# A spike-train feed-forward on one NeuronCore: 96 instead of 128 places for general tokens, and a second layer in which w2 stands still

## The chip, the core and the metric

The kernel runs on one core of a Trainium2 chip (trn2). The metric is device time in microseconds (us); a smaller number is better. Engines are named as the profile names them: PE is the matrix engine (TensorE), PEld its weight loads, DVE is VectorE, ACT is ScalarE, POOL is GpSimd, SP is SyncE, which here issues the plain transfers.

## The reference

The input x has 2 sequences of 2048 tokens and 512 channels. Each channel keeps a running sum; a spike of height 1000 stands where the sum passes a whole number. The spikes go through a two-layer network, and the result is added to x:

```
rates = relu(x) * 0.001
c     = cond[:, None, :] + cumsum(rates, axis=1)
spikes = (floor(c) - floor(previous c)) / 0.001
h     = relu(spikes @ w1 + b1)        # 512 -> 2048
out   = x + h @ w2 + b2               # 2048 -> 512
```

All data are float32. The sums here rise by less than two, so nearly all tokens have no spike at all, some have one, and few have several.

## The kernel before, in words

The kernel does not run the network over all 4096 tokens. It sorts tokens into three kinds.

**Idle tokens** have no spike. Their network output is one and the same row, `idle_row`; it is added to x in place by DVE and POOL (`add_idle`), and SP stores the result (`store_idle`).

**Single tokens** have one spike, in one channel. PE builds a table with the output row of every channel (`table_chunk`, 16 chunks of w1 and w2, a sum of 64 matmuls of 512 columns); POOL adds the rows onto the stored output with eight scattered accumulating transfers (`add_row`).

**General tokens** have spikes in several channels. DVE gives each of them a place, 1 to 128, in `hot` and `slot` (`find_slots`, `first_spikes`, `second_spikes`); PE then has the spikes of all places as `spk_t`, with 4 pieces of 128 channels on the partitions and the 128 places as columns. These places go through the network as one tile:

- `first_layer` on PE: for each of 16 pieces of 128 hidden units (`m`), 4 matmuls, w1 as the standing operand (128 by 128), the spikes as the moving one (128 columns). The results alternate between two PSUM tiles, `ps_turn` and `ps_small`; ACT turns each into `hidden[m]` (`relu_hidden`).
- `sum_checks` on PE, one small matmul with 2 moving columns: it counts the general tokens and odd cases for `judge` on DVE. If there were more general tokens than places, a slow loop over all tokens would follow (`redo`); it does not run on this input.
- `second_layer` on PE: 16 matmuls, `hidden[m]` as the standing operand and 512 columns of w2 as the moving one, summed in `ps_out`. The places stand on the partitions of the result, so that it can be used row by row.
- DVE adds x and b2 of those tokens (gathered by POOL into `general_x`) in one operation on `ps_out`, and POOL scatters the rows into the output.

The order on each engine is that of the code; there is no scheduler. Semaphores connect the engines: `spk_ready` (DVE to PE), `hidden_summed` and `hidden_ready` (PE to ACT and back), `out_summed` (PE to DVE), `row_ready` (DVE to POOL). SP ends the program when all stores and scatters have landed. The scatter names a row far outside the output for each empty place, and such rows are not written (`bounds_check`).

The last steps stand in the code like this:

```
            dve.wait_ge(out_summed, 1)
            dve.tensor_tensor(new_row, ps_out[:, :], general_x[:, :], ALU.add).then_inc(row_ready, 1)
...
            pool.wait_ge(row_ready, 1)
            pool.indirect_dma_start(out=out_rows, out_offset=bass.IndirectOffsetOnAxis(ap=to_general[:, :], axis=0),
```

The functions that the change touches, and what calls them:

Of the kernel before, what the change touches and what calls it, by code (L numbers as in the profile page):

```python
# [6 lines left out]
ALU = mybir.AluOpType  # L7
# [11 lines left out]
def spike_ffn(nc, x, x_turned, cond, cond_cols, w1, w_pairs, b1_cols, b2, out):  # L19
# [23 lines left out]
    NOT_FIRST = 1024.0  # L43
    assert BLK == 16 and D == 512 and B == 2 and F == 2048
# [10 lines left out]
    with ExitStack() as ctx:  # L55
# [22 lines left out]
        hot = sb("hot", [P, NE, P])  # L78
# [65 lines left out]
        new_row = w_sb[:, 8, 0, :]  # L144

# [27 lines left out]
        ps_checks = ps_table[DC - 1]  # L173

# [52 lines left out]
        hidden_ready = sem("hidden_ready")  # L227
        out_summed = sem("out_summed")
# [82 lines left out]
        def _(pool):  # L311
# [55 lines left out]
            for b in range(B):  # L367
                if b == 1:
                    pool.wait_ge(general_listed, 1)
                    pool.indirect_dma_start(out=general_x[:, :], out_offset=None, in_=x_rows,  # L370
                                            in_offset=bass.IndirectOffsetOnAxis(ap=from_general[:, :], axis=0)
                                            ).then_inc(general_got, 16)
# [8 lines left out]
            pool.indirect_dma_start(out=out_rows, out_offset=bass.IndirectOffsetOnAxis(ap=to_general[:, :], axis=0),  # L381
                                    in_=new_row, in_offset=None, bounds_check=last_row, oob_is_err=False
# [26 lines left out]
        def _(act):  # L409
# [40 lines left out]
            def relu_hidden(m, summed, count, ready):  # L450
                act.wait_ge(summed, count)
                act.activation(hidden[m], ps_hidden[m % 2][:, 0:P], ACT.Relu,  # L452
                               bias=b1_col[:, m:m + 1], scale=PER_DT).then_inc(ready, 1)

            for m in range(FC):
                relu_hidden(m, hidden_summed, m + 1, hidden_ready)
                if 1 <= m <= DC:
                    act.activation(table_row[m - 1], ps_table[m - 1][:, :], ACT.Copy).then_inc(table_rows_ready, 1)

            act.wait_ge(redo_ready, 1)  # L460
            redo = redo_count(act)
            with act.If(redo > 1):
                for b in range(B):
                    with act.Fori(1, redo) as tile:
# [3 lines left out]
                        for m in range(FC):  # L468
                            relu_hidden(m, again_hidden_summed, tile * FC + (b * BLK * FC - FC + m + 1),
                                        again_hidden_ready)  # L470
# [5 lines left out]
        def _(dve):  # L476
# [137 lines left out]
            def find_slots(b):  # L614
# [4 lines left out]
                chain(dve.tensor_tensor(hot[:, mine, :], over(slot[:, mine], P), along(slot_name[:, :], DC), ALU.is_equal))  # L619
# [7 lines left out]
            def first_spikes():  # L627
                dve.wait_ge(slots_found, 1)
                chain(dve.tensor_tensor(spk_t[:, :, :], over(token[:, own(0)], P), along(ps_slots[:, 0:P], DC), ALU.is_equal))  # L629

            def second_spikes():
                dve.wait_ge(slots_found, 2)
                for c in range(DC):
                    last = dve.scalar_tensor_tensor(out=spk_t[:, c, :], in0=ps_slots[:, P:2 * P],  # L634
                                                    scalar=token[:, DC + c:DC + c + 1], in1=spk_t[:, c, :],
# [17 lines left out]
            def list_general():  # L653
                for b in range(B):
                    chain(dve.scalar_tensor_tensor(out=diagonal[:, :], in0=ps_slots[:, b * P:(b + 1) * P], scalar=1.0,
                                                   in1=ident[:, :], op0=ALU.mult, op1=ALU.mult, accum_out=slot_rows[:, b:b + 1]))
                chain(dve.tensor_tensor(slot_row[:, :], slot_rows[:, 0:1], slot_rows[:, 1:2], ALU.add))
                chain(dve.tensor_scalar(none_far[:, :], slot_row[:, :], 0.5, FAR, ALU.is_lt, ALU.mult))
                dve.tensor_scalar(from_general[:, :], slot_row[:, :], -1.0, 0.0, ALU.add, ALU.max)
                dve.scalar_tensor_tensor(out=to_general[:, :], in0=slot_row[:, :], scalar=-1.0, in1=none_far[:, :],  # L660
                                         op0=ALU.add, op1=ALU.add).then_inc(general_listed, 1)

            def judge():
                dve.wait_ge(checks_summed, 1)
                chain(dve.tensor_scalar(crowd[:, :], ps_checks[:, 0:1], P + 0.5, None, ALU.is_gt))  # L665
# [61 lines left out]
            chain(dve.tensor_tensor(general_x[:, :], general_x[:, :], b2_row[:, :], ALU.add))  # L727
            dve.wait_ge(out_summed, 1)
            dve.tensor_tensor(new_row, ps_out[:, :], general_x[:, :], ALU.add).then_inc(row_ready, 1)  # L729
# [62 lines left out]
        def _(pe):  # L792
# [80 lines left out]
            def find_slots(b):  # L873
# [3 lines left out]
                for c in range(DC):  # L877
                    col = b * DC + c
                    last = pe.matmul(ps_slots[:, b * P:(b + 1) * P], token[:, col:col + 1].to_broadcast([P, P]),
# [3 lines left out]
            def first_layer(ready, base):  # L883
# [59 lines left out]
            with pe.If(redo > 1):  # L943
                pe.wait_ge(row_ready, 1)
                for b in range(B):
# [5 lines left out]
                    with pe.Fori(1, redo) as tile:  # L951
# [6 lines left out]
                        for last in first_layer(again_hidden_ready, base):  # L958
# [34 lines left out]
```

## Time and profile before

| | |
|---|---|
| time, three runs | 103.97, 103.45, 103.96 us; median 103.96 us |
| span of the profiled execution | 102.1 us; the timed runs are 1.3 to 1.9 us longer than this span |
| PE busy | 95.4 us (93% of the span), 370 records |
| PEld busy | 54.0 us (53%) |
| DVE busy | 65.9 us (64%) |
| ACT busy | 35.5 us (35%) |
| POOL busy | 43.2 us (42%) |
| mean granted TensorE clock | 0.991 |

The span runs from the first to the last instruction of the profiled execution; no separate device time is listed for that execution, so its span stands beside the runs. Each float32 matmul of the program leaves two records in the trace, each with a weight load of its own; a transpose leaves one. The end of a matmul record is modelled, so the distance from one start to the next says more of PE's pace than the length of a record.

### The profile page before, as it was taken

How to read it: one execution, taken by the hardware profiler on the slowest of the kernel's cores; microseconds unless marked ns; L12 is line 12 of the kernel's file. 1: busy time of each engine (PE TensorE's matmuls, PEld its weight loads, DVE VectorE, ACT ScalarE, POOL GpSimd, SP SyncE). 2: the span in 40 equal slices, each digit the busy share in tenths (PEclk: the TensorE clock that was granted, in tenths of full speed). 3: DMA queues.
4: the chain of work that ended last, by engine and by line, in shares of the span. 5: the costliest groups of instructions: out<-in, count | busy, mean ns of one | idle time of the engine just before them, and what ended most of it. 6: DMA issues, size and time to landing. Idle time of an engine off the chain costs nothing.

```text
span 102.1 us, 1157 instructions
## 1 busy us (share of the span) xinstructions
PE 95.4 (93%) x370; PEld 54.0 (53%) x370; DVE 65.9 (64%) x142; ACT 35.5 (35%) x64; POOL 43.2 (42%) x44
## 2 busy tenths in 40 slices
PE   5999999999999999999969999999999999999910
PEld 5944444444644444644234564649999984444300
DVE  2448999888699999488958888899993020020020
ACT  2796515315372540569740000003953330000000
POOL 6350000000078700017508181499937883688040
PEclk9999999999999999999999999999999999999996
DMA  1999999999999999999999725427999999998701
GB/s 58 286 387 414 417 420 411 411 407 409 409 409 409 396 393 401 409 394 387 379 373 352 324 116 218 193 125 292 395 430 436 407 336 195 218 115 106 92 8 62
DMA packets 10028, 31.66 MB, mean 310 GB/s; under 512 B 1671, under 2 KB 1799, under 8 KB 8994
## 3 DMA queue, kind: packets, MB, share of 16 engines
q1 hardware_dynamic: 8304, 29.63, 74.7%
q0 software_dynamic: 1568, 1.90, 11.4%
q8 instruction: 5, 0.08, 0.3%
q14 instruction: 5, 0.04, 0.1%
q10 hardware_dynamic: 146, 0.01, 0.1%
HBM read 21.58 MB, written 10.75 MB: 316 GB/s over the span
## 4 chain that ended last, share of the span: by engine, by line
PE 50%; DVE 20%; POOL 13%; issue 11%; ACT 1%; POOLq 1%; DVEq 0%
PE ps_table L807 40%; DVE x_sb L673 11%; POOL out L347 11%; PE ps_small L900 4%; DVE same L600 3%; PE ps_idle L823 2%; PE ps_turn L844 2%; DVE hot L619 1%; PE ps_idle L827 1%; PE ps_idle L833 1%; DVE spk_t L634 1%; POOL out L381 1%; POOL general_x L370 1%; POOLq L258 1%; DVE spk_t L629 1%
## 5 line engine op out<-in xcount | busy, mean ns | idle before, releaser
L807 PE MATMUL ps_table<-w_sb 128*128 128x512 f32 x128 | 56.9, 595 | 0.0
L807 PEld LDWEIGHTS ps_table<-w_sb 128*128 128x128 f32 x128 | 23.6, 190 | 27.1 <-issue 26.4
L342 POOL DMA_INDIRECT rates<-in_x_turned,sixteen_at x8 | 9.9, 1236 | 33.9 <-DVE sixteen_at L563 32.1
L354 POOL TENSOR_TENSOR x_sb<-x_sb,idle_row 128x512 f32<-128x512 f32 x12 | 14.9, 1277 | 9.9 <-DVEq L706 3.7
L422 ACT ACTIVATE w_sb<-w_sb,b_col 128x512 f32<-128x512 f32 (+2 forms) x19 | 12.2, 643 | 16.5 <-DMA w_sb<-in_w_pairs 16.3
L549 DVE SCALAR_TENSOR_TENSOR total_two<-x_sb,total_two 128x1024 f32<-128x1024 f32 x14 | 17.1, 1225 | 1.2 <-DMA x_sb<-in_x 0.8
L347 POOL DMA_INDIRECT out<-w_sb,to_single x8 | 12.5, 1558 | 5.8 <-issue 3.7
L895 PE MATMUL ps_table<-w_sb 128*128 128x512 f32 x32 | 14.0, 595 | 0.0
L423 ACT ACTIVATE w_sb<-w_sb,minus_relu_b 128x512 f32<-128x512 f32 (+2 forms) x19 | 12.3, 649 | 0.6
L673 DVE TENSOR_TENSOR x_sb<-x_sb,ps_idle 128x2048 f32<-128x2048 f32 x5 | 11.2, 2283 | 1.5 <-ACT idle_row L448 1.3
L895 PEld LDWEIGHTS ps_table<-w_sb 128*128 128x128 f32 x32 | 6.0, 190 | 7.2 <-issue 6.9
L452 ACT ACTIVATE w_sb<-ps_turn,b_col 128x128 f32<-128x128 f32 x8 | 2.9, 367 | 19.0 <-PE ps_turn L888 18.4
L888 PE MATMUL ps_small<-spk_t,w_sb 128*128 128x128 f32 x64 | 8.5, 275 | 0.0
L888 PE MATMUL ps_turn<-spk_t,w_sb 128*128 128x128 f32 x64 | 8.5, 275 | 0.0
L888 PEld LDWEIGHTS ps_turn<-spk_t,w_sb 128*128 128x128 f32 x64 | 7.9, 192 | 0.5 <-DVE spk_t L634 0.3
L888 PEld LDWEIGHTS ps_small<-spk_t,w_sb 128*128 128x128 f32 x64 | 7.8, 192 | 0.0
L509 DVE SCALAR_TENSOR_TENSOR idle_part<-w_sb,relu_b,idle_part 128x512 f32<-128x512 f32 x9 | 6.7, 750 | 1.5 <-DMA w_sb<-in_w_pairs 1.4
L729 DVE TENSOR_TENSOR w_sb<-ps_table,general_x 128x512 f32<-128x512 f32 x1 | 0.7, 692 | 6.3 <-PE ps_table L895 6.3
L900 PE MATMUL ps_small<-ones 128*128 128x128 f32 x16 | 3.7, 427 | 1.1 <-POOLq L320 1.1
L727 DVE TENSOR_TENSOR general_x<-general_x,b_row 128x512 f32<-128x512 f32 x1 | 0.7, 691 | 6.2 <-DMA general_x<-in_x,from_general 6.2
L900 PEld LDWEIGHTS ps_small<-ones 128*128 128x128 f32 x16 | 3.5, 330 | 1.1 <-POOLq L320 1.1
L665 DVE TENSOR_SCALAR crowd<-ps_table 128x1 f32<-128x1 f32 x1 | 0.2, 159 | 6.1 <-PE ps_table L871 6.1
(113 smaller groups left out, 65.5 us busy)
## 6 DMA issues: line engine op xcount, KB each, us to landing
x_sb<-in_x SPq DMA_DIRECT2D x16, 512.0 KB, 14.3
out<-x_sb SPq DMA_DIRECT2D x8, 1024.0 KB, 4.1
w_sb<-in_w_pairs SPq DMA_DIRECT2D x15, 512.0 KB, 15.7
w_sb<-in_w SPq DMA_DIRECT2D x4, 1024.0 KB, 15.3
w_sb<-in_w_pairs SPq DMA_DIRECT2D x2, 256.0 KB, 2.9
b_row<-in_b SPq DMA_DIRECT2D x1, 256.0 KB, 15.3
rates<-in_x_turned,sixteen_at POOLq DMA_INDIRECT x8, 6.5
out<-w_sb,to_single POOLq DMA_INDIRECT x8
```

What stands on the lines that cost most here:

```text
L342: pool.indirect_dma_start(out=rates[:, col, :], out_offset=None, in_=x_sixteen, in_offset=bass.IndirectOffsetOnAxis(ap=sixteen_at[:, col:c ...
L347: pool.indirect_dma_start(out=out_rows, out_offset=bass.IndirectOffsetOnAxis(ap=to, axis=0), in_=row, in_offset=None, bounds_check=last_ro ...
L354: last = pool.tensor_tensor(x_sb[b][:, t, :], x_sb[b][:, t, :], idle_row[:, :], ALU.add)
L422: chain(act.activation(weights, weights, ACT.Relu, bias=b1_col[:, m:m + 1], scale=PER_DT))
L423: act.activation(weights, weights, ACT.Identity, bias=minus_relu_b1[:, m:m + 1]).then_inc(table_hidden_ready, 1)
L509: step = dve.scalar_tensor_tensor(out=idle_part[:, :], in0=w2_sb[:, m, :], scalar=relu_b1[:, m:m + 1], in1=idle_part[:, :], op0=ALU.mult, ...
L549: chain(dve.scalar_tensor_tensor(out=total_two[b][:, :, :], in0=tokens, scalar=0.0, in1=total_two[b][:, :, :], op0=ALU.max, op1=ALU.add))
L673: last = dve.tensor_tensor(tokens, tokens, along(ps_idle[:, :], end - begin), ALU.add)
L807: last = pe.matmul(ps_table[c][:, :], table_hidden[:, m, c * P:(c + 1) * P], w2_sb[:, m, :], start=(m == 0), stop=(m == FC - 1))
L888: last = pe.matmul(ps_hidden[m % 2][:, 0:P], w1_sb[:, c, m * P:(m + 1) * P], spk_t[:, c, :], start=(c == 0), stop=(c == DC - 1))
L895: last = pe.matmul(ps_out[:, :], hidden[m], w2_sb[:, m, :], start=(m == 0), stop=(m == FC - 1))
L900: pe.matmul(ps_small[:, 0:P], ones[:, :], ones[:, :], start=True, stop=True)
```

## The change

General tokens get 96 places (`SLOTS`) instead of 128. Every operation on places has 96 columns or 96 partitions: `hot`, `spk_t`, the moving columns of `find_slots` and `first_layer`, `relu_hidden`, the gather into `general_x`, the list of rows, and the scatter. `judge` sends more than 96 general tokens into the slow loop.

The second layer is turned round. In `general_layer` a piece of w2 (128 hidden units by 128 output channels) stands still and `hidden[m]` moves with 96 columns: four sums of 16 matmuls, one for each 128 output channels, in four PSUM tiles. The results have the channels on the partitions. ACT copies each to `out_turned[c]`, and PE turns it back with a transpose (`turn_out`), three of them into `ps_out` and the last into another tile, `ps_out_last`. DVE adds x and b2 in two pieces of 384 and 128 channels.

```diff
+    SLOTS = 96
...
+        out_turned = [w_sb[:, 9, 0, c * SLOTS:(c + 1) * SLOTS] for c in range(DC)]
...
+        ps_out_turned = [ps_table[1], ps_table[2], ps_turn, ps_small]
+        ps_out_last = ps_table[1]
...
             for m in range(FC):
-                relu_hidden(m, hidden_summed, m + 1, hidden_ready)
+                relu_hidden(m, hidden_summed, m + 1, hidden_ready, SLOTS)
...
+            for c in range(DC):
+                act.wait_ge(out_turned_summed, c + 1)
+                act.activation(out_turned[c], ps_out_turned[c][:, 0:SLOTS], ACT.Copy).then_inc(out_turned_ready, 1)
...
-                chain(dve.tensor_tensor(hot[:, mine, :], over(slot[:, mine], P), along(slot_name[:, :], DC), ALU.is_equal))
+                chain(dve.tensor_tensor(hot[:, mine, :], over(slot[:, mine], SLOTS), along(slot_name[:, 0:SLOTS], DC), ALU.is_equal))
...
-            dve.wait_ge(out_summed, 1)
-            dve.tensor_tensor(new_row, ps_out[:, :], general_x[:, :], ALU.add).then_inc(row_ready, 1)
+            dve.wait_ge(out_summed, DC - 1)
+            most = slice(0, (DC - 1) * P)
+            chain(dve.tensor_tensor(new_row[0:SLOTS, most], ps_out[0:SLOTS, most], general_x[0:SLOTS, most], ALU.add))
+            dve.wait_ge(out_summed, DC)
+            rest = slice((DC - 1) * P, D)
+            dve.tensor_tensor(new_row[0:SLOTS, rest], ps_out_last[0:SLOTS, 0:P], general_x[0:SLOTS, rest], ALU.add).then_inc(
+                row_ready, 1)
...
-                        last = pe.matmul(ps_hidden[m % 2][:, 0:P], w1_sb[:, c, m * P:(m + 1) * P],
-                                         spk_t[:, c, :], start=(c == 0), stop=(c == DC - 1))
+                        last = pe.matmul(ps_hidden[m % 2][:, 0:n], w1_sb[:, c, m * P:(m + 1) * P],
+                                         spk_t[:, c, 0:n], start=(c == 0), stop=(c == DC - 1))
...
+            def turn_out(c):
+
+                pe.wait_ge(out_turned_ready, c + 1)
+                to = ps_out_last[0:SLOTS, 0:P] if c == DC - 1 else ps_out[0:SLOTS, c * P:(c + 1) * P]
+                pe.transpose(to, out_turned[c], ident[:, :]).then_inc(out_summed, 1)
+
+            def general_layer():
+
+                for c in range(DC):
+                    for m in range(FC):
+                        if c == 0:
+                            pe.wait_ge(hidden_ready, m + 1)
+                        last = pe.matmul(ps_out_turned[c][:, 0:SLOTS], w2_sb[:, m, c * P:(c + 1) * P], hidden[m][:, 0:SLOTS],
+                                         start=(m == 0), stop=(m == FC - 1))
+                    last.then_inc(out_turned_summed, 1)
+                    if c > 0:
+                        turn_out(c - 1)
+                turn_out(DC - 1)
...
-            for last in first_layer(hidden_ready, 0):
+            for last in first_layer(hidden_ready, 0, SLOTS):
                 last.then_inc(hidden_summed, 1)
             sum_checks()
-            second_layer(hidden_ready, 0).then_inc(out_summed, 1)
+            general_layer()
```

On PE, from the end of the first layer to the end of the second, the kernel before issues these rows (line, operation, the tile written and those read, partitions by columns, the semaphores waited for, how many in a row):

```order
L888 MATMUL ps_turn<-spk_t,w_sb 128x128 [waits hidden_ready]
L888 MATMUL ps_turn<-spk_t,w_sb 128x128 x3
L888 MATMUL ps_small<-spk_t,w_sb 128x128 [waits hidden_ready]
L888 MATMUL ps_small<-spk_t,w_sb 128x128 x3
L871 MATMUL ps_table<-checks,ones 128x2 [waits table_rows_ready,odd_ready]
L895 MATMUL ps_table<-w_sb 128x512 [waits hidden_ready] x16
```

The changed kernel issues these at the same place; the line numbers are its own, and `w_sb` holds w2, `hidden` and `out_turned`.

```order
L903 MATMUL ps_turn<-spk_t,w_sb 128x96 [waits hidden_ready]
L903 MATMUL ps_turn<-spk_t,w_sb 128x96 x3
L903 MATMUL ps_small<-spk_t,w_sb 128x96 [waits hidden_ready]
L903 MATMUL ps_small<-spk_t,w_sb 128x96 x3
L886 MATMUL ps_table<-checks,ones 128x2 [waits table_rows_ready,odd_ready]
L919 MATMUL ps_table<-w_sb 128x96 [waits hidden_ready] x16
L919 MATMUL ps_table<-w_sb 128x96 x16
L911 MATMUL ps_table<-ident,w_sb 96x128 [waits out_turned_ready]
L919 MATMUL ps_turn<-w_sb 128x96 x16
L911 MATMUL ps_table<-ident,w_sb 96x128 [waits out_turned_ready]
L919 MATMUL ps_small<-w_sb 128x96 x16
L911 MATMUL ps_table<-ident,w_sb 96x128 [waits out_turned_ready] x2
```

Sixteen matmuls with 512 columns became 64 with 96 columns and four transposes; two of the transposes stand between the sums, two behind the last.

On DVE, at the end of the program, the kernel before has these rows, from `judge` to the last addition:

```order
L666 TENSOR_TENSOR redo_f<-ps_table,crowd 128x1 [waits dve_step]
L667 TENSOR_SCALAR redo_f<-redo_f 128x1 [waits dve_step]
L668 TENSOR_SCALAR redo_i<-redo_f 128x1 [waits dve_step]
L727 TENSOR_TENSOR general_x<-general_x,b_row 128x512 [waits b2_in,general_got]
L729 TENSOR_TENSOR w_sb<-ps_table,general_x 128x512 [waits out_summed,dve_step]
```

The changed kernel has these there:

```order
L676 TENSOR_TENSOR redo_f<-ps_table,crowd 128x1 [waits dve_step]
L677 TENSOR_SCALAR redo_f<-redo_f 128x1 [waits dve_step]
L678 TENSOR_SCALAR redo_i<-redo_f 128x1 [waits dve_step]
L737 TENSOR_TENSOR general_x<-general_x,b_row 96x512 [waits b2_in,general_got]
L740 TENSOR_TENSOR w_sb<-ps_table,general_x 96x384 [waits out_summed,dve_step]
L743 TENSOR_TENSOR w_sb<-ps_table,general_x 96x128 [waits out_summed,dve_step]
```

The last addition is split in two, and only the second piece waits for the last transpose.

## Rows read from the trace of the kernel before

**Rows 1.** Busy time of each engine in three stretches, granted clock, DMA share.

```profile
core 0: us, PE busy (x) PEld busy (x) DVE busy (x) ACT busy (x) POOL busy (x), PEclk, DMA share, GB/s
...
68.50:83.20 14.70, 14.70 (x130) 14.46 (x129) 8.67 (x19) 7.47 (x19) 11.87 (x10) 1.00 0.97 391
83.20:97.40 14.20, 14.14 (x36) 6.14 (x34) 1.31 (x5) 0.37 (x1) 8.16 (x6) 1.00 0.89 153
97.40:102.10 4.70, 0.00 (x0) 0.00 (x0) 0.69 (x1) 0.00 (x0) 1.03 (x1) 0.80 0.10 37
```

**Rows 2.** Timeline of the last 5 us: start, length, engine, line, [idle before, releaser].

```profile
96.75 0.59 PE L895 MATMUL ps_table<-w_sb 128*128 128x512 f32 x1
97.45 0.69 DVE L729 TENSOR_TENSOR w_sb<-ps_table,general_x 128x512 f32<-128x512 f32 x1 [6.32 <-PE ps_table L895]
98.42 1.03 POOL L381 DMA_INDIRECT out<-w_sb,to_general  x1 [3.79 <-DVE w_sb L729]
```

**Rows 3.** Timeline of both layers on PE, PEld and POOL, merged runs of records.

```profile
68.52 0.19 PEld L888 LDWEIGHTS ps_turn<-spk_t,w_sb 128*128 128x128 f32 x1 [0.26 <-DVE spk_t L634]
68.93 1.05 PE L888 MATMUL ps_turn<-spk_t,w_sb 128*128 128x128 f32 x8
...
83.11 0.30 PEld L871 LDWEIGHTS ps_table<-checks,ones 128*128 128x128 f32 x2
83.22 0.28 PE L871 MATMUL ps_table<-checks,ones 128*128 128x2 f32 x2
83.33 0.30 PEld L895 LDWEIGHTS ps_table<-w_sb 128*128 128x128 f32 x2
83.36 13.98 PE L895 MATMUL ps_table<-w_sb 128*128 128x512 f32 x32
...
93.09 1.55 POOL L347 DMA_INDIRECT out<-w_sb,to_single  x1 [0.30 <-issue]
```

**Rows 4.** Timeline at `count_leads(1)`, where matmuls have one moving column.

```profile
62.23 1.02 PE L807 MATMUL ps_table<-w_sb 128*128 128x512 f32 x2
...
62.91 0.17 DVE L611 TENSOR_TENSOR_SCAN leads_run<-ones,leads 128x4 f32<-128x4 f32 x1
63.19 0.30 PEld L862 LDWEIGHTS ps_small<-leads_run,upper 128*128 128x128 f32 x2 [0.77 <-DVEq L612]
...
63.41 0.30 PEld L865 LDWEIGHTS ps_small<-leads_run,ones 128*128 128x128 f32 x2
63.63 0.30 PEld L807 LDWEIGHTS ps_table<-w_sb 128*128 128x128 f32 x2
```

**Rows 5.** The transposes of L856: duration ns min/median/max, first and last start.

```profile
L856 PEld LDWEIGHTS ps_met<-ident,token x4: 137/137/137, 47.2 to 47.9; 128*128 128x128 f32 x4
L856 PE MATMUL ps_met<-ident,token x4: 272/272/273, 47.7 to 48.0; 128*128 128x128 f32 x4
```

**Rows 6.** ACT by line and shape: busy us, mean ns of one.

```profile
L452 ACT ACTIVATE w_sb<-ps_small,b_col 128x128 f32<-128x128 f32 x8 | 2.9, 368 | 3.2 <-PE ps_small L888 2.6 <-issue 0.5
...
L458 ACT ACTIVATE w_sb<-ps_table 128x512 f32<-128x512 f32 x4 | 2.4, 590 | 0.0
...
L433 ACT ACTIVATE relu_b<-b_col 128x16 f32<-128x16 f32 x1 | 0.2, 216 | 0.4 <-DMA b_col<-in_b_cols 0.4
```

**Rows 7.** Timeline where PE waits for a copy of ACT.

```profile
51.34 0.60 ACT L446 ACTIVATE idle_base<-ps_idle 128x512 f32<-128x512 f32 x1 [0.91 <-PE ps_idle L827]
...
51.99 0.30 PEld L833 LDWEIGHTS ps_idle<-idle_base,strip_first 128*128 128x128 f32 x2 [1.63 <-ACT idle_base L446]
```

**Rows 8.** DVE by line and shape.

```profile
L619 DVE TENSOR_TENSOR hot<-slot,slot_name 128x512 f32<-128x512 f32 x2 | 1.4, 691 | 0.1
...
L665 DVE TENSOR_SCALAR crowd<-ps_table 128x1 f32<-128x1 f32 x1 | 0.2, 159 | 6.1 <-PE ps_table L871 6.1
```

**Rows 9.** DMA queue of POOL from 98.5 us to the end: packets, MB.

```profile
q0 software_dynamic: 80, 0.15, 10.8%
```

**Rows 10.** From the page's costliest groups, the first matmuls of the program.

```profile
L900 PE MATMUL ps_small<-ones 128*128 128x128 f32 x16 | 3.7, 427 | 1.1 <-POOLq L320 1.1
```

More of the change, by code:

```diff
@@ L77, in spike_ffn @@
         same = sb("same", [P, D], BF16)
-        hot = sb("hot", [P, NE, P])
+        hot = sb("hot", [P, NE, SLOTS])
         spk_t = sb("spk_t", [P, DC, P])
@@ L448, in _, with relu_hidden @@
             act.activation(idle_row[:, :], ps_idle[:, :], ACT.Copy).then_inc(idle_copied, 1)
[L450 removed]
+            def relu_hidden(m, summed, count, ready, n):
                 act.wait_ge(summed, count)
[L452 removed]
+                act.activation(hidden[m][:, 0:n], ps_hidden[m % 2][:, 0:n], ACT.Relu,
                                bias=b1_col[:, m:m + 1], scale=PER_DT).then_inc(ready, 1)
             for m in range(FC):
[L456 removed]
+                relu_hidden(m, hidden_summed, m + 1, hidden_ready, SLOTS)
                 if 1 <= m <= DC:
                     act.activation(table_row[m - 1], ps_table[m - 1][:, :], ACT.Copy).then_inc(table_rows_ready, 1)
+            for c in range(DC):
+                act.wait_ge(out_turned_summed, c + 1)
+                act.activation(out_turned[c], ps_out_turned[c][:, 0:SLOTS], ACT.Copy).then_inc(out_turned_ready, 1)
             act.wait_ge(redo_ready, 1)
@@ L628, in first_spikes @@
                 dve.wait_ge(slots_found, 1)
-                chain(dve.tensor_tensor(spk_t[:, :, :], over(token[:, own(0)], P), along(ps_slots[:, 0:P], DC), ALU.is_equal))
+                chain(dve.tensor_tensor(spk_t[:, :, 0:SLOTS], over(token[:, own(0)], SLOTS), along(ps_slots[:, 0:SLOTS], DC), ALU.is_equal))
             def second_spikes():
@@ L633, in second_spikes @@
                 for c in range(DC):
-                    last = dve.scalar_tensor_tensor(out=spk_t[:, c, :], in0=ps_slots[:, P:2 * P],
-                                                    scalar=token[:, DC + c:DC + c + 1], in1=spk_t[:, c, :],
+                    last = dve.scalar_tensor_tensor(out=spk_t[:, c, 0:SLOTS], in0=ps_slots[:, P:P + SLOTS],
+                                                    scalar=token[:, DC + c:DC + c + 1], in1=spk_t[:, c, 0:SLOTS],
                                                     op0=ALU.is_equal, op1=ALU.add)
@@ L878, in find_slots, with first_layer @@
                     col = b * DC + c
-                    last = pe.matmul(ps_slots[:, b * P:(b + 1) * P], token[:, col:col + 1].to_broadcast([P, P]),
+                    last = pe.matmul(ps_slots[:, b * P:b * P + SLOTS], token[:, col:col + 1].to_broadcast([P, P]),
                                      hot[:, col, :], start=(c == 0), stop=(c == DC - 1))
                 last.then_inc(slots_found, 1)
-            def first_layer(ready, base):
+            def first_layer(ready, base, n):
                 for m in range(FC):
@@ L957, in _ @@
                         base = tile * FC + (b * BLK * FC - FC)
-                        for last in first_layer(again_hidden_ready, base):
+                        for last in first_layer(again_hidden_ready, base, P):
                             last.then_inc(again_hidden_summed, 1)
```

29 lines of the change are left out of this document (16 added, 13 removed).

## The prediction

> **What bounds the kernel now.** I read the busy times by stretch first. From 68.5 to 97.4 us PE is busy in 28.84 of 28.9 us at a granted clock of 1.00, its full level; then it is silent, and DVE and POOL have one instruction each [rows 1]. The page's chain of work leads through POOL's single scatters instead; the timeline of the end corrects it. The last of these is issued at 93.09 and over at 94.64 [rows 3], but POOL's next scatter comes at 98.42 with an idle time put down to DVE's L729, which waited 6.32 us for PE's L895 [rows 2]. So the end is set by PE's two layers, then DVE's addition (97.45 to 98.14), then the last scatter. POOL has 94.64 to 98.14, 3.5 us, in hand.
>
> PE's first layer is not held up by what goes before on DVE: its first weight load, released by `spk_t`, starts at 68.52, and its first matmul at 68.93 [rows 3], a distance of 0.41 us, which is the length of the 512-column matmul still in the array (32 of them take 13.98 us to the end of the last [rows 3]; less 0.25 us of pipeline tail that is 0.43 each).
>
> **The price of a matmul with 96 columns** decides all. The rows give two candidates. By moving columns: a 512-column record takes 0.429 us, and a 128-column one (83.22 - 68.93) / 128 = 0.1116 us [rows 3]; the line through both gives 0.085 us at 96. By weight load: where the moving operand has one column (L862, L865), pairs of loads start at 63.19, 63.41 and 63.63, thus 0.11 us each [rows 4], and the two loads of L871 and those behind them, round matmuls of two columns, start 0.11 apart as well (83.11, 83.33) [rows 3]. Almost nothing moves there, and the pace is that of 128 columns. So a float32 load of 128 by 128 takes 0.111 us, one load runs beside one matmul, and 128 columns are just where both are equal. The change keeps every load at 128 by 128 and gives up only moving columns. I take 0.1115 us a record, with 0.109 as the low end (63.19 to 63.63 over four, read to 0.01 us, is 0.11).
>
> The Trainium skill (TensorE: Matmul & The Clock Gate, section Back-to-back issue gap) gives a rule for an isolated matmul in which the distance at full clock follows the moving columns with a small constant; by it one would go by the first candidate, and the sum below would be about 6 us lower on PE. The rows with one and two columns disagree with that here, since there is a weight load for every record; the page itself says that in a stream with loads both count.
>
> **First layer.** Same 128 records, same loads: 14.29 us before and after, gain 0. ACT's `relu_hidden` gets a little shorter (0.368 us at 128 columns [rows 6]) and is hidden, since a piece on PE lasts 8 x 0.1116 = 0.89 us. `find_slots` on PE also keeps its loads: 0.
>
> **Second layer.** Before: the stream takes 31 x 0.429 + 0.59 (the last record to its end) = 13.89 us from the first effective start at 97.34 - 13.89 = 83.45. (97.34 is 96.75 + 0.59 [rows 2]; the record itself starts at 83.36, ahead of its second load.) After: 64 matmuls, 128 records, 127 x 0.1115 = 14.16 us to the last start; two transposes stand among them, one record of 0.11 us each (four start between 47.7 and 48.0 [rows 5]), 0.22; and the last record to its end, 0.25 us (272 ns at 128 columns [rows 5], 32 fewer). Sum 14.63. **+0.74 us**; with 0.109 a record +0.42. The copies of the first three sums by ACT and their transposes lie under the next sum (16 x 2 x 0.1115 = 3.6 us): 0. All 16 `hidden` but the last are long ready.
>
> **Turning back, after the last sum ends.** Before: end of L895 at 97.34, DVE starts 0.11 later and takes 0.69: 0.80 us [rows 2]. After, two paths join. The last sum goes to ACT (0.04 us for the semaphore, my estimate, from the 0.05 between ACT's end at 51.94 and PE's load at 51.99 [rows 7]); a copy of 96 columns, which is between 216 ns (16 columns) and 368 ns (128 columns with a bias), by the line from 16 to 512 columns 0.28 us [rows 6]; 0.05 to PE [rows 7]; the transpose, 0.27 from matmul start to end plus about 0.06 of its load ahead (137 ns of record, half of it overlapping [rows 5]) = 0.33. Together 0.70. Meanwhile `turn_out(2)` comes 0.13 after the last sum; 0.11 later DVE starts on 384 columns, by the line from 159 ns for 1 to 691 for 512 columns [rows 8] 0.56 us, so it ends at 0.80. The last piece starts at about 0.81 by either path and takes 0.29 (128 columns on the same line): 1.10. **+0.30 us**; ends: copy 0.22 and all waits at their shortest +0.15; copy 0.37, and the chain's wait and the semaphores twice as long +0.65.
>
> **Start of the layers.** At 63.19 PE waits for DVE's `leads_ready`: its matmul L807 of 62.23 had streamed by 62.23 + 2 x 0.43 = 63.09, and the load of L862 starts 0.10 later and is not hidden [rows 4]. On DVE ahead of it stands `hot` for the first sequence, 4 x 128 columns in 691 ns [rows 8]; with 4 x 96 it is 128 x 1.04 = 0.13 us shorter. PE has about 0.10 of waiting and 0.11 of unhidden load to give back there. I take **-0.13 us**, from -0.20 to 0. The other shorter operations of DVE (`hot` for the second sequence, `spk_t`) finish `spk_t` some 0.4 us earlier, ahead of a PE that is the bound: 0.
>
> **The scatter.** It names 96 rows instead of 128, 1.03 us on POOL [rows 2]. No row shows one with fewer. If all of it goes by rows it is -0.26; if none, 0. **-0.10**, since the instruction has some fixed part. The transfer gains nothing: it moved 0.15 MB [rows 9], which is about 73 rows of 2 KB, so empty places are left out already, and it will be the same 73 rows. That number is also under 96, so the slow loop stays out. The gather for 96 rows ends long before it is needed: 0. Stores and single scatters have the 3.5 us in hand.
>
> **Sum.** +0.74 + 0.30 - 0.13 - 0.10 = +0.81 us. The profiled span of 102.1 becomes 102.9; the median of the runs, 103.96, lies 1.9 above the span, and I carry that over: **104.8 us**. With all terms at their ends the likeliest case goes from 103.96 + 0.42 + 0.15 - 0.20 - 0.26 = 104.1 to 103.96 + 0.74 + 0.65 = 105.4. What a measurement of this kernel can tell from no change is about 0.5%, 0.52 us, so "the same" is 103.4 to 104.5.
>
> **Rivals.**
> - *Moving columns set the pace.* Place: both layers. The first layer loses 128 x 0.0265 = 3.4 us; the second is 127 x 0.085 + 0.22 + 0.25 = 11.27 against 13.89, -2.6. The row would be ready about 5.8 us earlier, at 92.3; then POOL's last single scatter, over at 94.64, comes in between, and the gain ends at about 3.4 us: 100.5 us. It decides for faster as soon as a record falls below about 0.108 us in both layers. For it speaks that 0.1116 fits 128 columns as well; against it, all rows with one or two columns. 6 in 100.
> - *The clock falls.* PE then streams 96 columns in a record of 0.1115 us where it streamed 128, and no row shows what the clock does in such a stretch; it could be granted at its lower level, 1.2 GHz, in both layers. Against it: in this trace it fell only in the stretch in which PE is silent (0.80 on average [rows 1]), and the loads go on without a gap. The first matmuls of the program, of the same shape, took 3.7 us for 16 [rows 10], 0.23 each; at that price 256 records take 59 instead of 28.5 us: some 130 us. 2 in 100.
> - *The turned layer costs no more than it gives.* The same mechanism as the forecast, but the small gains are at their far ends (a scatter priced by rows, -0.26, PE's bubble fully gone, -0.20, a copy of 0.22 us): 104.1 to 104.5. 17 in 100.
>
> The forecast, load-bound with a sum over 0.52 us, keeps 75. Of the rivals the first is faster, the third the same, the second slower: faster 0.07 (with a little for an unseen gain), same 0.17, slower 0.76. The range of 104.0 to 105.5 is the likeliest case's own with its ends and 0.1 at either side, as the runs shown lie 0.5 us apart; it takes in the third rival. What is outside is the first two and terms that I have missed, together under 2 in 10.
>
> **What would show it.** In the changed profile the matmuls of the first layer should start 0.111 to 0.112 us apart, 8 in 0.89 us, as before; those of the second likewise, 16 matmuls in 3.57 us; PE's start of the first layer at about 68.8; the end of the last sum at about 97.95; ACT's copies of 0.25 to 0.37 us; the last transpose some 0.7 us behind the last sum; DVE's last piece at an end of about 99.05; the scatter 0.9 to 1.03 us. The prediction is wrong if a load with 96 moving columns behind it goes faster than one with 1 or 128, if the clock row shows less than 1.00 between 68 and 98 us, or if transposes among the matmuls hold up the stream by more than their 0.11 us.

## The result and the profile after

The changed kernel took 105.58 us (median; 105.17 to 105.86), beside 103.97 us for the kernel before: ratio 1.0171, interval 1.0111 to 1.0232. Three later comparisons of the same two kernels gave 1.0126 (1.0070 to 1.0182), 1.0108 (1.0070 to 1.0147) and 1.0111 (1.0049 to 1.0173). Ratios leave out slow executions (here one of the kernel before, of 207.75 us), which the medians, here and below, take in. The change makes the kernel 1.1 to 1.7% slower; 0.8 us, 0.8%, was forecast, with a range that ended at 105.5 us. The profiled execution has its own time here, 105.17 us, with a span of 103.4 us.

The stretches of the changed kernel that answer to [rows 1], cut where its own layers begin and end (busy us and number of records of each engine, granted clock, DMA share, GB/s):

```profile
68.50:82.80 14.30, 14.30 (x130) 14.30 (x129) 7.94 (x19) 7.07 (x19) 12.08 (x9) 1.00 0.97 388
82.80:98.50 15.70, 15.23 (x136) 14.82 (x134) 1.95 (x7) 1.35 (x5) 7.34 (x6) 1.00 0.76 127
98.50:103.40 4.90, 0.00 (x0) 0.00 (x0) 0.21 (x1) 0.00 (x0) 0.99 (x1) 0.82 0.16 42
```

The clock stays at its full level through both layers. The first layer takes 14.3 us as before (83.22 - 68.93 = 14.29 [rows 3]). The stretch of the second, which now holds the turning back and most of DVE's addition too, is 15.7 us long instead of 14.2, and the silent end 4.9 instead of 4.7, although POOL's scatter has become a little shorter. The records of the two layers show the pace; these are the lines of the first and second layer in the changed kernel (duration ns min/median/max, first and last start):

```profile
L903 PE MATMUL ps_turn<-spk_t,w_sb x64: 246/275/275, 68.5 to 81.8; 128*128 128x96 f32 x64
...
L919 PEld LDWEIGHTS ps_turn<-w_sb x32: 190/192/192, 90.1 to 93.6; 128*128 128x128 f32 x32
L919 PE MATMUL ps_turn<-w_sb x32: 248/275/275, 90.2 to 93.7; 128*128 128x96 f32 x32
```

A sum of 32 records starts its first load at 90.14 and the transpose behind it is loaded at 93.68 (next fence); that is 0.111 us a record with 96 moving columns, the price of a 128-column record in [rows 3]. The timeline of the end, which answers to [rows 2]:

```profile
90.14 3.65 PEld L919 LDWEIGHTS ps_turn<-w_sb 128*128 128x128 f32 x32
...
93.68 0.15 PEld L911 LDWEIGHTS ps_table<-ident,w_sb 128*96 128x96 f32 x1
...
93.90 3.71 PE L919 MATMUL ps_small<-w_sb 128*128 128x96 f32 x32
...
97.44 0.27 PE L911 MATMUL ps_table<-ident,w_sb 128*96 128x128 f32 x1
97.64 0.25 ACT L467 ACTIVATE w_sb<-ps_small 128x96 f32<-128x96 f32 x1 [3.40 <-PE ps_small L919]
97.83 0.56 DVE L740 TENSOR_TENSOR w_sb<-ps_table,general_x 96x384 f32<-96x384 f32 x1 [7.28 <-PE ps_table L911]
97.95 0.13 PEld L911 LDWEIGHTS ps_table<-ident,w_sb 128*96 128x96 f32 x1 [0.46 <-ACT w_sb L467]
97.95 0.32 PE L911 MATMUL ps_table<-ident,w_sb 128*96 128x128 f32 x1 [0.23 <-ACT w_sb L467]
98.42 0.29 DVE L743 TENSOR_TENSOR w_sb<-ps_table,general_x 96x128 f32<-96x128 f32 x1
98.98 0.99 POOL L387 DMA_INDIRECT out<-w_sb,to_general  x1 [4.84 <-DVE w_sb L743]
```

The row is finished at 98.42 + 0.29 = 98.71, which is 30.21 us behind the first matmul of the first layer (68.50). Before it was 98.14 - 68.93 = 29.21 [rows 2, 3]. The layers and the turning back cost **1.0 us**; 1.04 was forecast. But from the row to the end of the span it now takes 103.4 - 98.7 = 4.7 us instead of 102.1 - 98.1 = 4.0: **0.7 us** that the prediction did not have. The scatter, issued at 98.98, lands (its last data have arrived) 3.4 us later, instead of 2.7:

```profile
q0 software_dynamic: 64, 0.15, 12.1%
q8 instruction: 2, 0.03, 3.5%
q14 instruction: 3, 0.02, 1.7%
issues: line engine op xcount, KB each, median us to landing
out<-w_sb,to_general POOLq DMA_INDIRECT x1, 3.4
```

This is the view of DMA queues from 98.9 us to the end. The scatter moves the same 0.15 MB as in [rows 9]. What is new is queue q8, which carries instructions. The same view of 99.7 to 99.9 us places the first of its two packets:

```profile
q8 instruction: 1, 0.02, 42.5%
```

42.5% of 16 engines over 0.2 us are 1.4 us for this packet, to about 101.1. All 64 packets of q0 start between 100.5 and 102.0, so that it lies beside the scatter's data. The second packet starts behind 102.5, when the scatter has landed. The reason stands in the rows of PE's sequencer (PEldq), which the page does not count as busy: the reading of `redo`, and the branch over the slow loop. First those of the changed kernel,

```profile
L977 PEldq COMPARE_BRANCH  x1: 3694/3694/3694, 98.8 to 98.8; - x1
...
L264 PEldq TENSOR_LOAD <-redo_i x1: 484/484/484, 97.9 to 97.9; - x1
```

then those of the kernel before:

```profile
L943 PEldq COMPARE_BRANCH  x1: 3631/3631/3631, 90.4 to 90.4; - x1
...
L258 PEldq TENSOR_LOAD <-redo_i x1: 535/535/535, 89.5 to 89.5; - x1
```

The branch takes 3.7 us now and took 3.6 before. Before, PE's sequencer had run ahead of its matmuls and took it at 90.4, under 7 us of queued work; the branch was over at 94.0. Now the last transpose waits for ACT, the sequencer waits with it, and the branch begins at 98.8, beside the scatter, and ends at 102.49. The Trainium skill (Advanced Engine Details and Errata, section Control Flow Timing) gives some 108 ns for a compare-and-branch; the branches over the same loop on ACT, POOL and DVE took 45, 53 and 72 ns in this trace, but PE's took 3.7 us, so the measurement decides for PE. The Trainium skill (Runtime: NRT & Kernel Launch, section Instruction fetch mechanics) says that code is fetched in blocks of 16 KiB over a DMA queue of its own, in sequence; the 0.03 MB in two packets on q8 agree with that size.

### The profile page after: what moved, and what is told of

It reads as the page before. It is cut to its first block, busy times and chain, and to the rows that moved or that the text cites. A ratio compares the mean times of both kernels' runs of the same rounds, so it can differ in the third digit from the quotient of the medians.

```text
span 103.4 us, 1363 instructions
## 1 busy us (share of the span) xinstructions
PE 96.9 (94%) x470; PEld 63.0 (61%) x470; DVE 65.5 (63%) x143; ACT 36.0 (35%) x68; POOL 43.2 (42%) x44
## 4 chain that ended last, share of the span: by engine, by line
PE 60%; POOL 13%; issue 11%; DVE 11%; POOLq 1%; DVEq 0%
PE ps_table L822 50%; POOL out L353 11%; DVE x_sb L683 9%; PE ps_small L934 4%; PE ps_idle L838 2%; PE ps_turn L859 2%; POOL out L387 1%; POOL general_x L376 1%; DVE spk_t L643 1%; PE ps_idle L848 1%; PE ps_met L894 1%; POOLq L264 1%; DVE hot L628 1%; PE ps_turn L871 0%; PE ps_met L871 0%
## 5 line engine op out<-in xcount | busy, mean ns | idle before, releaser
L822 PE MATMUL ps_table<-w_sb 128*128 128x512 f32 x128 | 57.6, 601 | 0.0
L822 PEld LDWEIGHTS ps_table<-w_sb 128*128 128x128 f32 x128 | 24.0, 193 | 27.6 <-issue 27.3
L458 ACT ACTIVATE w_sb<-ps_turn,b_col 128x96 f32<-128x96 f32 x8 | 2.7, 342 | 19.0 <-PE ps_turn L903 18.9
L903 PE MATMUL ps_small<-spk_t,w_sb 128*128 128x96 f32 x64 | 8.5, 275 | 0.0
L903 PE MATMUL ps_turn<-spk_t,w_sb 128*128 128x96 f32 x64 | 8.4, 275 | 0.0
L919 PE MATMUL ps_table<-w_sb 128*128 128x96 f32 x64 | 7.4, 276 | 0.0
L919 PEld LDWEIGHTS ps_table<-w_sb 128*128 128x128 f32 x64 | 7.2, 192 | 0.0
L740 DVE TENSOR_TENSOR w_sb<-ps_table,general_x 96x384 f32<-96x384 f32 x1 | 0.6, 555 | 7.3 <-PE ps_table L911 7.3
L737 DVE TENSOR_TENSOR general_x<-general_x,b_row 96x512 f32<-96x512 f32 x1 | 0.7, 687 | 6.0 <-DMA general_x<-in_x,from_general 6.0
```

Source lines behind the costliest of these rows:

```text
L822: last = pe.matmul(ps_table[c][:, :], table_hidden[:, m, c * P:(c + 1) * P], w2_sb[:, m, :], start=(m == 0), stop=(m == FC - 1))
L903: last = pe.matmul(ps_hidden[m % 2][:, 0:n], w1_sb[:, c, m * P:(m + 1) * P], spk_t[:, c, 0:n], start=(c == 0), stop=(c == DC - 1))
L919: last = pe.matmul(ps_out_turned[c][:, 0:SLOTS], w2_sb[:, m, c * P:(c + 1) * P], hidden[m][:, 0:SLOTS], start=(m == 0), stop=(m == FC - 1))
```

## The experiments

Two theories stood against each other for the missing 0.7 us. **Theory A**: PE's late branch; its code fetch delays the scatter, or PE's own end sets the end. **Theory B**: the scatter of 96 rows itself lands late.

**PE's loop and branch taken out.** The edit is the same in both kernels: PE's part of the slow loop goes, with the reading of `redo`.

```diff
-            pe.wait_ge(redo_ready, 1)
-            redo = redo_count(pe)
-            with pe.If(redo > 1):
-                pe.wait_ge(row_ready, 1)
...
             pe.sem_inc(passed, 1)
```

The changed kernel without it:

> The changed kernel with the slow loop taken out of PE's program alone (the loop does not run on this input; with it PE's reading of redo and its branch over the loop are gone). Theory A: the missed term is PE's branch, which now waits for the last transpose, takes 3.7 us to fetch code, and fetches it while the last scatter lands. Then PE ends with its last transpose, the last scatter lands 1.6 to 1.8 us behind the end of POOL's instruction instead of 2.4, and the time falls by 0.7 to 1.3 us against the changed kernel, to 104.3 to 104.9. Theory B: the scatter of 96 rows itself lands late, since its rows spread less evenly over the engines of the transfer: no fall, 105.2 to 105.9, landing 2.4 us as before.

The kernel before without it:

> The kernel before with the slow loop taken out of PE's program alone, the control of the run beside it. Theory A: PE's branch there ran at 90.4 to 94.0 us under the queued matmuls, so nothing is gained: within 0.3 us of the kernel before. If less code alone makes a kernel faster, it falls by as much as the changed kernel does, 0.7 us or more.

The control stayed where it was, 103.84 beside 103.54 us (1.0023, 0.9986 to 1.0061). In the changed kernel the end became nearly as short as before: 4.1 us from the row to the end, landing 2.8 us, in its three profiles. This is the end of the timeline of such a profile, of the run repeated later, with a span of 102.1 us:

```profile
97.71 0.29 DVE L743 TENSOR_TENSOR w_sb<-ps_table,general_x 96x128 f32<-96x128 f32 x1
98.28 0.99 POOL L387 DMA_INDIRECT out<-w_sb,to_general  x1 [6.01 <-DVE w_sb L743]
```

The DMA view of the same profile from 97.9 us to the end:

```profile
q0 software_dynamic: 64, 0.15, 12.4%
q14 instruction: 3, 0.02, 1.8%
issues: line engine op xcount, KB each, median us to landing
out<-w_sb,to_general POOLq DMA_INDIRECT x1, 2.8
```

Queue q8 is empty in this stretch. The 64 packets of the scatter are the same, but all of them start within 1.0 us (99.8 to 100.8) instead of 1.5, and they land 0.6 us earlier. Theory B falls. The time did not follow as clearly: 104.91 beside 103.54 us (1.0125, 1.0064 to 1.0186), the same ratio as the changed kernel's on another chip, where 0.7 us less was expected. More runs on this stand below.

**The 96 places alone**, with the old second layer; ACT's copies go, and DVE adds in one operation again.

```diff
-            general_layer()
+            second_layer(hidden_ready, 0, SLOTS).then_inc(out_summed, 1)
...
-                    last = pe.matmul(ps_out[:, :], hidden[m], w2_sb[:, m, :], start=(m == 0), stop=(m == FC - 1))
+                    last = pe.matmul(ps_out[0:n, :], hidden[m][:, 0:n], w2_sb[:, m, :], start=(m == 0), stop=(m == FC - 1))
```

> 96 places, but the second layer as before (hidden stands still, w2 moves with 512 columns). Theory A: the second layer's stream is the old one, 13.9 us, PE reads redo early as before, the landing is as before; the gain is 0.13 us of start and some 0.04 us of POOL: 103.6 to 104.0, ratio 0.996 to 1.001. Theory B: the scatter of 96 rows lands 0.7 us later here too: 104.4 to 104.8.

Measured: 103.58 beside 103.54 us, 0.9997 (0.9962 to 1.0033). The scatter of 96 rows lands 2.8 us after its issue and takes 0.99 us on POOL (1.03 with 128 rows [rows 2]). The places by themselves are worth nothing that can be measured, and do not delay the landing.

**The kernel before with a late branch**: PE waits for its own last matmul, and reads `redo` then.

```diff
+            pe.wait_ge(out_summed, 1)
             pe.wait_ge(redo_ready, 1)
             redo = redo_count(pe)
```

> The kernel before with one wait added on PE: it reads redo only when its own last matmul has ended (out_summed). Theory A: the branch starts at about 98.3 us of the span, takes 3.6 us, and its fetch meets the last scatter: the landing takes 2.2 us or more instead of 1.7, PE's end comes at about 102, and the time rises by 0.5 to 1.3 us, to 104.5 to 105.3. Theory B: nothing on the path changes, within 0.3 us of the kernel before.

Measured: 104.41 beside 103.54 us, 1.0065 (1.0023 to 1.0108). With nothing else changed, one wait brought the whole picture. This is the row of the branch in its profile:

```profile
L944 PEldq COMPARE_BRANCH  x1: 3371/3371/3371, 97.9 to 97.9; - x1
```

And this is the last scatter among its DMA issues (count, us to landing), where the kernel before has 2.7:

```profile
out<-w_sb,to_general POOLq DMA_INDIRECT x1, 3.6
```

**The changed kernel with the branch after the scatter**, a single execution:

```diff
+            pe.wait_ge(general_scattered, 16)
             pe.wait_ge(redo_ready, 1)
```

> The changed kernel with PE's reading of redo held back until the last scatter has landed. It tells apart the two ways in which the late branch can cost: by its fetch beside the scatter, or by PE's own end. Theory A1 (the fetch delays the scatter): the scatter lands 1.3 to 1.5 us behind POOL's instruction, as in the kernel before, instead of 2.0; PE then ends some 4.3 us later, and the whole time is 3.5 us or more above the changed kernel's. Theory A2 (only PE's end counts): the landing stays at 2.0 us.

It took 108.03 us, span 106.2. The row of the branch (start 102.4, 3.3 us):

```profile
L978 PEldq COMPARE_BRANCH  x1: 3334/3334/3334, 102.4 to 102.4; - x1
```

The DMA view from 98.7 to 101.9 us:

```profile
q0 software_dynamic: 64, 0.15, 16.4%
q14 instruction: 3, 0.02, 2.6%
issues: line engine op xcount, KB each, median us to landing
out<-w_sb,to_general POOLq DMA_INDIRECT x1, 2.8
```

The scatter, without q8 beside it, landed in 2.8 us. So the fetch delays the scatter (A1). The figures of the expectation were not met as they stand: the landing came 1.8 us behind POOL's instruction, by the same views 1.7 in the kernel before and 2.4 in the changed one, and the time was 3.3 us above the 104.71 us of the changed kernel on the same chip (below).

PE's end counts as well: here, moved behind the scatter, it alone sets the end. In the changed kernel it does not. Each engine ends with a row `DRAIN`; these are POOL's and PE's there,

```profile
L56 POOLq DRAIN  x1: 3954/3954/3954, 99.2 to 99.2; - x1
...
L56 PEldq DRAIN  x1: 8/8/8, 102.7 to 102.7; - x1
```

and this is POOL's in the kernel before:

```profile
L55 POOLq DRAIN  x1: 3214/3214/3214, 98.7 to 98.7; - x1
```

POOL's ends 0.8 us behind the landing of the scatter in both: at 99.2 + 4.0 = 103.2 behind 98.98 + 3.4 = 102.4, and at 101.9 behind 98.42 + 2.7 = 101.1. PE is through 0.5 us before POOL in the changed kernel, at 102.7. So there the late landing sets the end. With the landing back at 2.8 us POOL would be through at about 102.6 (an estimate, 98.98 + 2.8 + 0.8), and PE, at 102.7, would keep only some 0.1 us of the delay.

**The turned layer alone**, with 128 places (one number, `SLOTS = 128`).

> The turned second layer with 128 places, all operations on places as wide as before. Theory A (weight loads set the pace): both layers keep 0.1116 us a record, so that the time is that of the changed kernel within 0.4 us, 104.9 to 105.9, and 30.2 to 30.4 us lie between the first layer's start and the row. Rival (moving columns set the pace, or part of it): 128 columns cost more than 96, by 256 x 0.0265 = 6.8 us at most.

Measured: 105.36 beside 103.37 us, 1.0201 (1.0141 to 1.0261). In its profile 30.3 us lie between the first layer's start and the row, as expected, and 4.5 us between the row and the end; the scatter, beside a late branch here too, landed in 3.2 us. The changed kernel, again, on the same chip:

> The changed kernel once more, for a second profile and a time on the chip of the runs beside it. Theory A: 29.2 us from the first layer's start to the finished row become 30.2, and the time from there to the end is 4.6 to 5.0 us instead of 4.0; ratio to the kernel before 1.012 to 1.022. Theory B, by which the late landing was chance of one profile: 4.0 us to the end, ratio 1.006 to 1.011.

104.71 us, 1.0126 (1.0070 to 1.0182), 4.7 us from the row to the end, landing 3.4. So the late landing was not chance: all four profiles of the changed kernel have one of 3.4 to 3.6 us. The run with 128 places took 0.65 us more than this one, where at most 0.4 was expected; its profile, of an execution of 104.75 us, does not show where that goes, and it stays open. The turned layer has the same pace with 128 columns as with 96. These are its lines with 128 places:

```profile
L919 PEld LDWEIGHTS ps_turn<-w_sb x32: 190/192/192, 89.8 to 93.3; 128*128 128x128 f32 x32
L919 PE MATMUL ps_turn<-w_sb x32: 275/275/275, 89.9 to 93.4; 128*128 128x128 f32 x32
```

31 distances in 3.5 us, as above with 96. The 6.8 us of the rival are not there.

**Loads half as wide**: w2 in pieces of 128 by 64, eight sums, 96 moving columns; a single execution.

```diff
-                for c in range(DC):
+                for q in range(2 * DC):
...
-                        last = pe.matmul(ps_out_turned[c][:, 0:SLOTS], w2_sb[:, m, c * P:(c + 1) * P], hidden[m][:, 0:SLOTS],
+                        last = pe.matmul(ps_out_turned[q % DC][0:HALF, 0:SLOTS],
+                                         w2_sb[:, m, q * HALF:(q + 1) * HALF], hidden[m][:, 0:SLOTS],
```

> The changed kernel with w2 in pieces of 128 by 64 instead of 128 by 128: eight sums instead of four, each load half as wide, 96 moving columns as in the changed kernel. Theory A (a record lasts as long as the longer of its load and its stream, and 128-column loads were the longer one): a record of the second layer falls from 0.1116 to some 0.085 us, that of 96 moving columns; 256 records then take 21.7 us instead of 14.3, the time is 7 to 8 us above the changed kernel's. Rival (a record of this size costs 0.11 us whatever is loaded, as an issue cost): 0.1116 stays, 28.6 us, the time 14 us above.

It took 113.28 us, span 111.4, some 8.2 us above the changed kernel on that chip (105.08, below), a little more than expected. The loads lasted 137 ns instead of 192, and a sum, from its first matmul to the transpose behind it,

```profile
87.90 2.85 PE L922 MATMUL ps_turn<-w_sb 128*64 128x96 f32 x32
90.69 0.26 PE L915 MATMUL ps_table<-ident,w_sb 64*96 64x64 f32 x1
```

took 2.79 us, 0.087 a record. So 96 columns move in 0.087 us or less when the load is short, and with a full load the load sets the pace. The issue-cost rival (0.1116 whatever is loaded) falls.

**How much of the late branch reaches the time.** The changed kernel and the one without PE's branch on one chip, twice:

> The changed kernel, on one chip with the run without PE's branch, since the profiles put 0.64 us between their ends (4.71 and 4.72 against 4.08 us from the row to the end) and the medians, taken on different chips, do not. Theory A: 1.2 to 1.8 us above the kernel before, and 0.4 to 0.9 us above the run without PE's branch. Rival: the two lie within 0.2 us of each other, and the late branch shows in profiles only.

> The changed kernel without PE's slow loop and branch, on the same chip as the changed kernel. Theory A: 0.7 to 1.2 us above the kernel before, 0.4 to 0.9 us under the changed kernel. Rival: as long as the changed kernel within 0.2 us.

> The changed kernel, beside the next run on one chip. Theory A (the late branch counts in full): 1.3 to 1.8 us above the kernel before and 0.5 to 0.8 us above the run without PE's branch. Theory C (it counts in part, since the start of the layers varies and something before them is later): 0.1 to 0.4 us above that run.

> The changed kernel without PE's slow loop and branch. Theory A: 0.8 to 1.1 us above the kernel before, the price of the turned layer alone. Theory C: 1.1 to 1.4 us above it, with the first layer's start no earlier than in the kernel before.

| on the chip of | kernel before | changed | changed, no PE branch | before, late branch |
|---|---|---|---|---|
| the third comparison | 103.69 us | 105.08, 1.0108 (1.0070 to 1.0147) | 104.88, 1.0087 (1.0043 to 1.0132) | |
| the fourth comparison | 103.79 us | 104.87, 1.0111 (1.0049 to 1.0173) | 104.12, 1.0050 (1.0013 to 1.0087) | 104.34, 1.0051 (1.0018 to 1.0085) |

The last column is the repeat of the kernel before with the late branch:

> The kernel before with PE's branch held back to the end of its last matmul, once more. Theory A: 0.6 to 1.0 us above the kernel before, with 4.7 to 5.0 us from the row to the end. Theory C: 0.2 to 0.5 us above it.

Its landing was 3.7 us, and 5.0 us lay between row and end. By the ratios the branch is worth 0.2% on one chip and 0.6% on the other in the changed kernel, and 0.65% and 0.5% in the kernel before: some 0.2 to 0.7 us, where the profiles show 0.6 to 1.0. The first run of the changed kernel without the branch, on the chip of the fourth comparison, showed none of it (1.0125 above, beside 1.0111 of the changed kernel). That the late branch costs time is shown in the kernel before (neither interval reaches 1); its full size in the time is not settled: the first layer's start moves by a microsecond from execution to execution (67.8 to 69.1 us over the profiles, with no order by kernel), which may hide the rest.

**A faster version.** The second layer as before, hidden standing still, but in two sums of 384 and 128 columns, so that DVE adds the first part under the second sum; with 96 places and with 128.

```diff
+                for n, cols in enumerate((slice(0, (DC - 1) * P), slice((DC - 1) * P, D))):
+                    for m in range(FC):
+                        if n == 0:
+                            pe.wait_ge(hidden_ready, m + 1)
+                        to = ps_out[0:SLOTS, cols] if n == 0 else ps_out_last[0:SLOTS, 0:P]
+                        last = pe.matmul(to, hidden[m][:, 0:SLOTS], w2_sb[:, m, cols],
+                                         start=(m == 0), stop=(m == FC - 1))
+                    last.then_inc(out_summed, 1)
```

> 96 places, hidden stands still as before, but the second layer in two sums of 384 and 128 columns of w2, so that DVE adds the first 384 channels under the second sum. Theory A: the stream gets some 0.15 us longer (16 x 2 more records with a fixed part of 4.5 ns), the last addition 0.40 us shorter: 28.9 to 29.0 us from the first layer's start to the row instead of 29.2, PE's branch stays early, the end as before: 0.2 to 0.4 us below the kernel before, ratio 0.995 to 0.999. Rival (more records and a second semaphore cost as much): ratio 1.000 or more.

> The second layer with hidden standing still, in two sums of 384 and 128 columns, with 128 places. It tells whether the gain of that split needs the 96 places. Theory A: nearly all of it comes from the split: 28.9 to 29.0 us from the first layer's start to the row, 0.1 to 0.3 us below the kernel before. Rival (the places make it): 29.2 us and the time of the kernel before.

With 96 places: 103.04 beside 103.37 us, 0.9965 (0.9931 to 0.9998): well under the changed kernel on the same chip (1.0126) and 0.3% under the kernel before, with 1 just outside the interval. With 128: 103.65 beside 103.69 us, 0.9988 (0.9947 to 1.0030), unclear. The end of the timeline with 96 places:

```profile
94.28 2.35 PE L910 MATMUL ps_table<-w_sb 128*96 128x128 f32 x20
...
96.74 0.29 DVE L740 TENSOR_TENSOR w_sb<-ps_table,general_x 96x128 f32<-96x128 f32 x1 [2.93 <-PE ps_table L910]
```

With 128 places:

```profile
94.99 2.29 PE L910 MATMUL ps_table<-w_sb 128*128 128x128 f32 x19
...
97.38 0.29 DVE L740 TENSOR_TENSOR w_sb<-ps_table,general_x 128x128 f32<-128x128 f32 x1 [3.01 <-PE ps_table L910]
```

PE's branch did not stay as early as the expectation had it. With 96 places it starts 5 us later than in the kernel before,

```profile
L965 PEldq COMPARE_BRANCH  x1: 3529/3529/3529, 95.4 to 95.4; - x1
```

and is over at 98.9, behind the scatter's issue at 97.30. The scatter landed in 2.8 us all the same (2.9 with 128 places): the packets of q8 start at about 96.4 and 99.7, those of the scatter between 98.8 and 99.8, with 128 places at 97.2 and 100.7 beside 99.5 to 100.4. What delays a scatter is a fetch in the time of its data, and here both fetches just miss it.

Both versions add only 128 columns behind the last matmul, in 0.29 us where L729 took 0.69 [rows 2]. The row comes 28.9 us (first layer at 68.16 by the trace, row at 97.03) and 29.0 us (68.70, 97.67) after the first layer's start, 0.2 to 0.3 us earlier than in the kernel before. Most of the gain of the path is the split's; whether the places add to it is inside the intervals.

## Why the prediction was wrong, point by point

- **The price of a matmul with 96 columns**: right. 0.111 us a record in both layers; 128 columns have the same pace, half loads have 0.087. Of the sentences that the prediction took from the Trainium skill (TensorE: Matmul & The Clock Gate, section Back-to-back issue gap), the rule by moving columns does not hold here, where each record has a load of its own; that in a stream with loads both count agrees. Only with the narrow load does a record come near the prediction's price by moving columns (0.087 us beside 0.085).
- **First layer 0, second layer +0.74**: right. The first layer takes 14.3 us. The last sum ends at 93.90 + 3.71 = 97.61, 29.11 us behind the first matmul of the first layer; before it was 97.34 - 68.93 = 28.41, so that both layers together cost +0.70. (The 0.25 us that the prediction calls a tail are 0.16 of tail, 0.59 - 0.43, and 0.09 of a slower start; no term hangs on it.)
- **Turning back, +0.30**: right. From the end of the last sum to the row it takes 98.71 - 97.61 = 1.10 us instead of 0.80. ACT's copy took 0.25 us (forecast 0.28), DVE's pieces 0.56 and 0.29 as forecast; layers and turning back together cost 1.0 us (forecast 1.04).
- **Start of the layers, -0.13**: right at its place, but not to be seen in the time. These are the rows of the changed kernel's timeline there:

```profile
61.48 1.45 PE L822 MATMUL ps_table<-w_sb 128*128 128x512 f32 x3
...
62.76 0.30 PEld L877 LDWEIGHTS ps_small<-leads_run,upper 128*128 128x128 f32 x2 [0.66 <-DVEq L621]
...
63.20 0.30 PEld L822 LDWEIGHTS ps_table<-w_sb 128*128 128x128 f32 x2
```

  The load waited 0.66 us for DVE instead of 0.77. From the start of the last record ahead of it (61.48 + 2 x 0.43 = 62.34) to the load of the table's next matmul (63.20) went 0.86 us, before it was 0.97 (62.66 to 63.63 [rows 4]): a gain of 0.11. In the time it cannot be seen: the places alone have a ratio of 0.9997 (0.9962 to 1.0033).
- **The scatter, -0.10**: too large a gain. POOL's instruction went from 1.03 to 0.99 us. That the transfer moves the same rows was right, the packets are 0.15 MB in both.
- **What failed** is the step on the end. "Turning back" put waits for ACT on PE, and the prediction followed them to DVE and POOL, but did not ask what is queued behind them on PE itself: the reading of `redo` and a branch of 3.7 us, which stand in the code right behind the second layer and in the trace of before at 90.4 us. The sentence "the transfer gains nothing" left out that it could lose: its landing went from 2.7 to 3.4 us, and the landing sets the end. That is a term of +0.6 to +1.0 us in the profiles and of some +0.2 to +0.7 in the times, shown by the late branch in the kernel before and by the landing without the branch; the prediction had it at nothing.
- **The sum**: 1.0 + 0.7 us in the profile, from the first layer's first matmul on, against 0.81 forecast (1.04 less 0.23 of small gains). The profiled spans differ by 1.3 us, since the first layer started 0.4 us earlier in the changed kernel's profile (68.50 against 68.93). Of that 0.1 is the change's; the rest is the spread from execution to execution: in the kernel before without PE's branch, whose code is the same up to there, it started at 67.9.
- **The rivals**: the clock stayed at 1.00 in both layers, the moving columns did not set the pace, and the turned layer cost more than it gave.

Open is why the first comparison came out at 1.7% and the three later ones at 1.1 to 1.3%; their intervals overlap. So is the 0.65 us of the turned layer with 128 places.

## What to carry to other kernels

Before a stationary and a moving operand are exchanged, count the loads: here a float32 record lasted as long as the longer of its weight load (0.111 us for 128 columns) and its stream, so fewer moving columns than 128 gave nothing back. When a wait is put on an engine, look at everything behind it in that engine's own order, control flow too: a branch that is free under queued work can delay the end when it comes last, here by 0.6 to 1.0 us in the profiles. And a final addition can be split so that only a small piece of it follows the last matmul, without touching the matmul's shape.

## What the runs showed of the hardware that was not expected

- PE's branch over the slow loop took 3.3 to 4.0 us in every profile that has it, wherever it stood, while the branches over the same loop on ACT, POOL and DVE took 45 to 72 ns in the changed kernel.
- One code fetch of PE, a packet of 0.02 MB, in the time of the data of a scatter of 0.15 MB moved the landing of that scatter from 2.7 to 2.9 us to 3.2 to 3.7; a fetch just ahead of or behind the data did not.
- The start of the first layer varied by about a microsecond between profiles of kernels that are alike up to there (67.9 to 68.9 us in those with 128 places), more than most of the terms that the prediction weighed.
